# Weighing the values of two key tiles in a row in a causal attention stage

## The chip, the cores and the metric

One core of one Trainium2 chip. The metric is the device time of one execution in microseconds (us); the profiled execution has its own time, and its span runs from its first to its last instruction.

## The reference, cut to what matters

Sixteen-head causal attention over 4 sequences of 1024 tokens with 256 features (16 per head), a residual and a layer norm, then a mixture of 16 experts with two picks per token and a shared expert, a residual and a second norm. All of it is float32. The change touches the attention alone:

```python
q = split_heads(x @ Wq + bq)
k = split_heads(x @ Wk + bk)
v = split_heads(x @ Wv + bv)
scores = jnp.einsum('bhqd,bhkd->bhqk', q, k) / jnp.sqrt(jnp.float32(dk))
scores = jnp.where(causal[None, None], scores, -jnp.inf)
attn = jax.nn.softmax(scores, axis=-1)
out = jnp.einsum('bhqk,bhkd->bhqd', attn, v)
```

## The kernel before, in words

The kernel has three blocks, one after the other, each with its own instruction stream per engine: the projections to queries, keys and values (lines 377 to 577), the attention (lines 580 to 798), and all that follows (from line 812).

Attention runs in 16 steps: one per sequence (4) and group of four heads (4). A step works on two halves of 512 queries (`qc`), and each half on the key tiles of 128 that it may see (`kt`): 4 for the first half, 8 for the second. That makes 12 units (`UNITS`, line 39), numbered 0 to 11. Units 0 to 3 and 8 to 11 lie on the diagonal, so that their widths are 512, 384, 256 and 128 columns; units 4 to 7 are 512 wide.

For each unit there are

- the scores (line 722), in two pairs of heads: keys as weights, queries streaming, bfloat16, into PSUM banks 0 to 3, one bank per head. Every unit uses the same four banks, so a pair waits until the exp has read the same pair of the unit before (line 727);
- the exp on ScalarE (line 656), one activation per pair of heads, from PSUM into a slot of `probs` in SBUF. There are `PSLOTS` slots, and an exp waits until the weighing that last used its slot is done (line 659);
- for units on the diagonal the mask on GpSimd (line 628);
- the weighing (line 733): the probabilities stream, in float32, against the values of the four heads, each 32 columns wide (16 values and ones for the sum). Each head writes its own 32 partitions of bank 6, so the four run beside each other in the array; the trace shows this form as `128*32`. A half's weighings add up in bank 6, and then ScalarE copies them out (`copy_out`, line 666), TensorE turns the copy (`turn_out`, line 761) and VectorE divides by the sum (`normalise`, line 687).

The maximum that the exp subtracts is worked out one step ahead, beside this: TensorE computes the scores in a second arrangement, queries as weights (`piece_scores`, line 317, the matmuls of line 323 and on the diagonal the mask by line 326), and VectorE reduces each piece (`piece_maximum`, line 337). There are 38 pieces per step (`MAXES`, lines 45 to 51), numbered 0 to 37. When a half's pieces are reduced, VectorE splits the maxima into three bfloat16 parts (`max_parts`, line 349), TensorE turns these (`turn_maxima`, line 329), VectorE copies them (`copy_maxima`, line 344) and a DMA puts them as three further rows under the queries (`load_max`, line 370). Pieces and both kinds of turn share three PSUM banks, 4, 5 and 7, one after the other in the order in which they come (`RING_USERS`, line 94): each waits until the third one before it has been read (`ring_free`, line 748).

Each engine takes its own instructions strictly in order. TensorE's order in a step is written by `attention_order` (line 62): a chain of scores and weighings, in which the pieces of maxima are placed as their share of the cost comes due, and the turns are put behind certain items. VectorE takes the ring's users in the same order (line 698). A unit's weighing comes behind the next unit's scores. The last step has no next step, so it has neither pieces nor their turn for the first half (`present`, line 102). SyncE's queue carries `load_max` and the loads of queries and keys two steps ahead (line 600).

In memory, `probs` lies in `work` (line 581), and behind its three slots the third of three sets of values (line 296). The tensor `wgu` is free during the attention (its weights come later), and the third set of queries and keys and a block of zeros lie in it (lines 279 and 582).

Of the kernel before, what the change touches and what calls it, by code (L numbers as in the profile page):

```python
# [6 lines left out]
F32 = mybir.dt.float32  # L7
# [12 lines left out]
GH = 4  # L20
# [18 lines left out]
UNITS = [(qc, kt) for qc in range(HALVES) for kt in range(CT * (qc + 1))]  # L39
NU = len(UNITS)  # L40
DIAG = [u for u, (qc, kt) in enumerate(UNITS) if kt >= CT * qc]
PSLOTS = 3


MAXES = []
# [16 lines left out]
def attention_order():  # L62

    main = [("scores", 0, 0), ("scores", 0, 1), ("weigh", -1, 0)]
    for u in range(NU - 1):
        main += [("scores", u + 1, 0), ("scores", u + 1, 1), ("weigh", u, 0)]
    cost = [unit_width(u) * (2 if what == "weigh" else 1) for what, u, _ in main]  # L70
    pieces = [m[2] * m[4] + 60 for m in MAXES]
    order, n, done, spent = [], 0, 0, 0
    for item, c in zip(main, cost):
        order.append(item)
        if item == ("scores", 1, 1):
            order.append(("turn_max", 1, 0))
        if item == ("weigh", 1, 0):
            order.append(("turn_out", 1, 0))
        if item == ("weigh", 5, 0):
            order.append(("turn_out", 0, 0))  # L80
        done += c
        while n < NM and (spent + pieces[n] / 2) / sum(pieces) <= done / sum(cost):
            order.append(("max", n, 0))
            spent += pieces[n]
            n += 1
            if n == NM0 + TURN_AFTER:
                order.append(("turn_max", 0, 0))
    assert n == NM
    return order
# [113 lines left out]
def build(nc, x, xT, Wq, bq, Wk, bk, Wv, bv, Wo, bo, gate_w, expert_bias, sg_w, su_w, sd_w, gu_w, down_w, out):  # L203
    with ExitStack() as ctx:
# [87 lines left out]
                                 .rearrange("(h d) t -> d h t", d=DK)).then_inc(stack_loaded[r], 16)  # L292

        held = ctx.enter_context(ExitStack())
        vg = [held.enter_context(nc.sbuf_tensor(f"vg{r}", [P, NT, GH, 32], F32)) for r in range(2)]
        vg.append(work[:, 6144:7168].rearrange("p (t h e) -> p t h e", t=NT, h=GH))
        oT = [held.enter_context(nc.sbuf_tensor(f"oT{r}", [P, CH], F32)) for r in range(2)]
        mT = [held.enter_context(nc.sbuf_tensor(f"mT{r}", [3 * GH, CH], BF16)) for r in range(2)]
        recip = held.enter_context(nc.sbuf_tensor("recip", [P, CT, GH], F32))
        m_neg = held.enter_context(nc.sbuf_tensor("m_neg", [P, NT, GH], F32))  # L300
        m_neg_late = held.enter_context(nc.sbuf_tensor("m_neg_late", [P, CT, GH], F32))
# [278 lines left out]
        with ExitStack() as c2:  # L580
# [73 lines left out]
            @blk.scalar  # L654
            def _(act):
                def exp(i, u):
                    off = CH - unit_width(u)
                    s = (u % PSLOTS) * GH
                    wait_count(act, pv_done, NU * i + u - PSLOTS + 1)
                    for pair in range(2):  # L660
                        act.wait_ge(score_ready, 2 * (NU * i + u) + pair + 1)
                        act.activation(probs[:, s + 2 * pair:s + 2 * pair + 2, off:CH],  # L662
                                       ps[:, SCORE_BANK + 2 * pair:SCORE_BANK + 2 * pair + 2, off:CH],
                                       ACT.Exp, scale=float(DK) ** -0.5).then_inc(exp_done, 1)

                def copy_out(i, qc):
                    act.wait_ge(pv_done, NU * i + (CT if qc == 0 else NU))
                    wait_count(act, oT_ready, 2 * i + qc - 1)
                    act.activation(oT[qc][:, :], ps[:, OUT_BANK, :], ACT.Copy).then_inc(o_copied, 1)

                def step(i, prev=True):
                    for u in range(NU):
                        exp(i, u)
                        if u == 0 and prev:
                            copy_out(i - 1, 1)
                        if u == CT:
                            copy_out(i, 0)

                step(0, prev=False)
                step(1)  # L680
                with act.Fori(2, STEPS) as i:
                    step(i)
                copy_out(STEPS - 1, 1)
# [35 lines left out]
            @blk.tensor  # L719
            def _(pe):  # L720

                def scores(i, r, u, pair):
                    qc, kt = UNITS[u]
                    off = CH - unit_width(u)
                    if pair == 0 and kt == 0:
                        pe.wait_ge(m_loaded[qc], 48 * i + 48)
                    wait_count(pe, exp_done, 2 * (NU * i + u) + pair - 1)
                    for h in (2 * pair, 2 * pair + 1):
                        mm = pe.matmul(ps[:, SCORE_BANK + h, off:CH], ks[r][0:KM, h, kt * P:(kt + 1) * P],  # L729
                                       qs[r][0:KM, h, qc * CH + off:(qc + 1) * CH], start=True, stop=True)  # L730
                    mm.then_inc(score_ready, 1)

                def weigh(i, r, u):
                    qc, kt = UNITS[u]
                    off = CH - unit_width(u)
                    s = (u % PSLOTS) * GH
                    if u in DIAG:
                        pe.wait_ge(masked, len(DIAG) * i + DIAG.index(u) + 1)
                    else:
                        pe.wait_ge(exp_done, 2 * (NU * i + u) + 2)  # L740
                    if kt == 0:
                        wait_count(pe, o_copied, 2 * i + qc)
                    for h in range(GH):
                        mm = pe.matmul(ps[32 * h:32 * h + 32, OUT_BANK, off:CH], vg[r][:, kt, h, :],  # L744
                                       probs[:, s + h, off:CH], start=(kt == 0), stop=(kt == CT * (qc + 1) - 1))
                    mm.then_inc(pv_done, 1)

                def ring_free(i, item, first, last, second=False):

                    before, ago = ring_before(item, first, last, second)  # L750
                    if before is None:
                        return
                    what, n, _ = before
                    if what == "max":
                        wait_count(pe, reduced, NM * (i + 1 - ago) + n + 1)
                    elif what == "turn_max":
                        wait_count(pe, mT_copied[n], i + 2 - n - ago)
                    else:
                        wait_count(pe, a_written, 2 * (i - ago) + (1 if n == 0 else 0))

                def turn_out(i, qc):
                    pe.wait_ge(o_copied, 2 * i + qc + 1)
                    for t in range(CT):
                        mm = pe.transpose(ps[:, ring_bank(("turn_out", qc, 0)), t * P:(t + 1) * P],
                                          oT[qc][:, t * P:(t + 1) * P], ident[:, :])
                    mm.then_inc(oT_ready, 1)

                def step(i, k3, r, first=False, last=False, second=False):
                    pe.wait_ge(vg_ready, i + 1)
                    for item in ORDER:  # L770
                        what, n, pair = item
                        if item == ("max", 0, 0) and not last:
                            pe.wait_ge(stack_loaded[(r + 1) % STACKS], 192 * (k3 + (r + 1) // STACKS) + 192)
                        if what == "scores":
                            scores(i, r, n, pair)
                        elif what == "weigh":
                            if n >= 0:
                                weigh(i, r, n)
                            elif not first:
                                weigh(i - 1, (r - 1) % STACKS, NU - 1)  # L780
                        elif present(item, first, last):
                            ring_free(i, item, first, last, second)
                            if what == "max":
                                piece_scores(pe, i + 1, (r + 1) % STACKS, n, ring_bank(item))
                            elif what == "turn_max":
                                turn_maxima(pe, i + 1 - n, n, ring_bank(item))
                            else:
                                turn_out(i - n, n)

                step(0, 0, 0, first=True)  # L790
                step(1, 0, 1, second=True)
                pe.wait_ge(ones_ready, 2 * STACKS)
                for i in range(2, STEPS - 1):
                    step(i, i // STACKS, i % STACKS)
                step(15, 5, 15 % STACKS, last=True)
                weigh(STEPS - 1, 15 % STACKS, NU - 1)
                pe.wait_ge(a_written, 2 * STEPS - 1)
                turn_out(STEPS - 1, 1)

# [752 lines left out]
```

## Time and profile before

| | us |
|---|---|
| median of 3 runs | 989.87 (989.46 to 995.76) |
| the profiled execution, its own time | 996.05 |
| its span | 994.0 |
| TensorE busy in the span | 859.3 |
| VectorE busy | 643.4 |
| ScalarE busy | 474.3 |
| GpSimd busy | 341.1 |

The profile shows one execution. Times in it are counted from the span's start. The matmuls are pipelined: a matmul's record ends when its last result is through the array, later than the next one may start, so the distance between two starts, the pitch, is what a matmul costs its engine. The granted clock is the share of the TensorE clock's full speed.

### The profile page before, as it was taken

The numbers are of one execution on the slowest core, as the hardware profiler recorded it, in microseconds if no ns is written. First come the engines' busy times: TensorE is split into PE (matmuls) and PEld (weight loads), VectorE is DVE, ScalarE is ACT, GpSimd is POOL, SyncE is SP. The second block draws the span as 40 slices with busy tenths as digits, with TensorE's granted clock in tenths as the row PEclk, the third lists the DMA queues.
The fourth block names the chain that finished last, engine by engine and source line by source line (L and its number), as shares of the span: only waits on it lengthen the run. The fifth ranks groups of instructions, "written<-read, shape, count | busy, mean of one in ns | idle before, by whom it ended". The sixth has DMA issues, their size and how long they took to land. (4 is left out here: it accounts for less than half of the span.)

```text
span 994.0 us, 17348 instructions
## 1 busy us (share of the span) xinstructions
PE 859.3 (86%) x5476; PEld 482.8 (49%) x5477; DVE 643.4 (65%) x1527; ACT 474.3 (48%) x712; POOL 341.1 (34%) x450
## 2 busy tenths in 40 slices
PE   7979799999999999999999997978388669999910
PEld 4635444444444444444444426964157448878700
DVE  6428788888888888888888823882391112227655
ACT  3423366666666666666656673643112223444312
POOL 3513311221111221112211125637434655556732
PEclk9979899999999999999999998998598789999965
DMA  9874757555776556555224004602214434558563
GB/s 281 193 209 133 144 65 120 73 102 100 124 130 93 88 103 106 65 66 66 40 39 53 2 1 128 213 0 102 91 38 130 124 122 144 151 189 247 199 211 127
DMA packets 90410, 114.62 MB, mean 115 GB/s; under 512 B 9200, under 2 KB 70896, under 8 KB 90352
## 3 DMA queue, kind: packets, MB, share of 16 engines
q1 hardware_dynamic: 75728, 86.79, 41.5%
q0 software_dynamic: 7680, 21.11, 5.8%
q10 hardware_dynamic: 6944, 5.93, 1.9%
q8 instruction: 38, 0.62, 0.3%
q14 instruction: 20, 0.16, 0.1%
HBM read 62.74 MB, written 50.66 MB: 114 GB/s over the span
## 5 line engine op out<-in xcount | busy, mean ns | idle before, releaser
L662 ACT ACTIVATE work<-ps 128x1024 f32<-128x1024 f32 (+3 forms) x384 | 293.8, 811 | 180.0 <-PE ps L729 179.8
L341 DVE TENSOR_REDUCE m_neg<-ps 128x1 f32<-128x512 f32 (+3 forms) x432 | 265.2, 662 | 23.8 <-PE ps L326 13.4
L633 POOL TENSOR_SCALAR_AFFINE_SELECT work<-work 128x512 f32<-128x512 f32 x128 | 81.5, 637 | 386.5 <-ACT work L662 386.5
L323 PE MATMUL ps<-stacks 96*128 96x512 bf16 (+3 forms) x528 | 151.0, 330 | 1.5 <-DVE m_neg L341 1.5
L729 PE MATMUL ps<-stacks 99*128 99x512 bf16 (+3 forms) x528 | 124.7, 329 | 6.2 <-PEq L377 4.6
L341 DVE TENSOR_REDUCE m_neg_late<-ps 128x1 f32<-128x384 f32 (+3 forms) x176 | 106.7, 636 | 26.5 <-PE ps L326 26.5
L1029 POOL DMA_INDIRECT z_back<-stacks,home x96 | 93.4, 972 | 77.6 <-issue 30.6
L744 PE MATMUL ps<-work,vg 128*32 128x512 f32 (+3 forms) x1056 | 112.5, 498 | 1.5 <-POOL work L633 1.4
L1464 PE MATMUL ps<-wgu,work 128*128 x384 | 98.9, 404 | 8.6 <-issue 5.9
L1289 DVE TENSOR_TENSOR work<-work,ps 128x256 f32<-128x256 f32 x48 | 20.2, 420 | 130.3 <-ACT work L1111 101.4
L326 PE MATMUL ps<-mask_b,ident_b 128*128 128x128 bf16 x512 | 99.6, 221 | 0.0
L323 PEld LDWEIGHTS ps<-stacks 96*128 96x128 bf16 x528 | 49.6, 97 | 95.0 <-DVE m_neg L341 50.5
L1464 PEld LDWEIGHTS ps<-wgu,work 128*128 128x128 f32 x384 | 74.7, 205 | 19.2 <-issue 9.8
L1021 POOL DMA_INDIRECT y_sorted<-v_home,row_of x64 | 63.0, 984 | 43.4 <-DVE row_of L1256 23.9
L558 PE MATMUL ps<-work,wqk 128*128 128x512 f32 x128 | 63.5, 641 | 12.5 <-DMA work<-in_xT 7.0
L323 PE MATMUL ps<-wgu 96*128 96x512 bf16 (+3 forms) x240 | 68.8, 329 | 0.0
L729 PEld LDWEIGHTS ps<-stacks 99*128 99x128 bf16 x528 | 44.2, 98 | 43.8 <-ACT work L662 11.1
L447 POOL TENSOR_TENSOR work<-work 128x512 bf16<-128x512 f32 x32 | 36.7, 1156 | 71.6 <-ACT work L480 71.6
L729 PE MATMUL ps<-wgu 99*128 99x512 bf16 (+3 forms) x240 | 56.3, 325 | 0.0
L326 PEld LDWEIGHTS ps<-mask_b,ident_b 128*128 128x128 bf16 x512 | 50.7, 99 | 10.8 <-issue 2.5
L1480 PE MATMUL ps<-wdn,work 128*128 x192 | 51.1, 390 | 0.2
L744 PE MATMUL ps<-work 128*32 128x512 f32 (+3 forms) x480 | 51.1, 498 | 0.0
(142 smaller groups left out, 1075.8 us busy)
## 6 DMA issues: line engine op xcount, KB each, us to landing
stacks<-qk_parts SPq DMA_DIRECT2D x132, 128.0 KB, 6.4
y_sorted<-wgu SPq DMA_DIRECT2D x8, 1560.0 KB, 10.5
work<-y_sorted SPq DMA_DIRECT2D x48, 260.0 KB
qk_parts<-work SPq DMA_DIRECT2D x32, 384.0 KB, 2.9
work<-z_back SPq DMA_DIRECT2D x32, 256.0 KB
wgu<-qk_parts SPq DMA_DIRECT2D x60, 128.0 KB, 6.7
work<-in_xT SPq DMA_DIRECT2D x8, 512.0 KB, 5.3
work<-in_x SPq DMA_DIRECT2D x8, 512.0 KB, 4.2
```

Source lines behind the costliest of these rows:

```text
L323: mm = pe.matmul(dst, qs[r][0:KS, h0 + m, qt * P:(qt + 1) * P], ks[r][0:KS, h0 + m, half * CH:half * CH + w], start=True, stop=not diag)
L326: mm = pe.matmul(dst[:, w - P:w], ident_b[:, :], mask_b[:, :], start=False, stop=True)
L341: dve.tensor_reduce(dst, ps[:, bank, 0:heads * w].rearrange("p (h k) -> p h k", h=heads), AX.X, ALU.max, negate=True).then_inc(reduced, 1)
L558: mm = pe.matmul(ps[:, t, :], wqk[:, t // 2, h, (t % 2) * P:(t % 2 + 1) * P], xt[half][:, h, :], start=(h == 0), stop=(h == DC - 1))
L633: pool.affine_select(out=blk_, in_=blk_, compare_op=ALU.is_ge, fill=0.0, base=0, pattern=[[0, GH], [1, P]], channel_multiplier=-1).then_in ...
L662: act.activation(probs[:, s + 2 * pair:s + 2 * pair + 2, off:CH], ps[:, SCORE_BANK + 2 * pair:SCORE_BANK + 2 * pair + 2, off:CH], ACT.Exp, ...
L729: mm = pe.matmul(ps[:, SCORE_BANK + h, off:CH], ks[r][0:KM, h, kt * P:(kt + 1) * P], qs[r][0:KM, h, qc * CH + off:(qc + 1) * CH], start=Tr ...
L744: mm = pe.matmul(ps[32 * h:32 * h + 32, OUT_BANK, off:CH], vg[r][:, kt, h, :], probs[:, s + h, off:CH], start=(kt == 0), stop=(kt == CT * ...
L1021: pool.indirect_dma_start(out=y_sorted[g], out_offset=bass.IndirectOffsetOnAxis(ap=row_of[:, j, t:t + 1], axis=0), in_=y_rows_all[:, t, :] ...
L1029: pool.indirect_dma_start(out=z_back, out_offset=bass.IndirectOffsetOnAxis(ap=home[:, 2 * n + k:2 * n + k + 1], axis=0), in_=zs[n % ZS][:, ...
L1464: mm = pe.matmul(ps[:, 2 + r, 2 * F * k:2 * F * (k + 1)], ysT[r][:, h, k, :], wgu[:, bass.ds(e, 1), h, :].squeeze(1), start=(h == 0), stop ...
L1480: mm = pe.matmul(ps[:, 6 + r, D * k:D * (k + 1)], hxT[r][:, k, :], wdn[:, bass.ds(e, 1), :].squeeze(1), start=True, stop=True)
```

## The change

TensorE's order goes by pairs of units: the scores of units u and u+1, and then the weighings of units u-2 and u-1, one straight behind the other. No ring user is placed between the two weighings. So that exps of four units can be held, `probs` has four slots; the third set of values, which lay behind it, gets its own tensor, and the second output copy and the second buffer of turned maxima move into `wgu`. ScalarE's output copies come one exp later. What is left over at the end of a step is now two weighings, and the next step takes them.

```diff
-PSLOTS = 3
+PSLOTS = 4
...
-    main = [("scores", 0, 0), ("scores", 0, 1), ("weigh", -1, 0)]
-    for u in range(NU - 1):
-        main += [("scores", u + 1, 0), ("scores", u + 1, 1), ("weigh", u, 0)]
+    main = []
+    for u in range(0, NU, 2):
+        main += [("scores", u, 0), ("scores", u, 1), ("scores", u + 1, 0), ("scores", u + 1, 1),
+                 ("weigh", u - 2, 0), ("weigh", u - 1, 0)]
     cost = [unit_width(u) * (2 if what == "weigh" else 1) for what, u, _ in main]
     pieces = [m[2] * m[4] + 60 for m in MAXES]
     order, n, done, spent = [], 0, 0, 0
     for item, c in zip(main, cost):
         order.append(item)
+        done += c
+        if item[0] == "weigh" and item[1] % 2 == 0:
+            continue
         if item == ("scores", 1, 1):
             order.append(("turn_max", 1, 0))
...
-        done += c
         while n < NM and (spent + pieces[n] / 2) / sum(pieces) <= done / sum(cost):
...
-        vg = [held.enter_context(nc.sbuf_tensor(f"vg{r}", [P, NT, GH, 32], F32)) for r in range(2)]
-        vg.append(work[:, 6144:7168].rearrange("p (t h e) -> p t h e", t=NT, h=GH))
-        oT = [held.enter_context(nc.sbuf_tensor(f"oT{r}", [P, CH], F32)) for r in range(2)]
-        mT = [held.enter_context(nc.sbuf_tensor(f"mT{r}", [3 * GH, CH], BF16)) for r in range(2)]
+        vg = [held.enter_context(nc.sbuf_tensor(f"vg{r}", [P, NT, GH, 32], F32)) for r in range(STACKS)]
+        wgu_words = wgu[:, :, :, :].rearrange("p e c n -> p (e c n)")
+        oT = [held.enter_context(nc.sbuf_tensor("oT0", [P, CH], F32)),
+              wgu_words[:, GH * N + TRASHES * ROW:GH * N + TRASHES * ROW + CH]]
+        mT_at = GH * N + TRASHES * ROW + CH
+        mT = [held.enter_context(nc.sbuf_tensor("mT0", [3 * GH, CH], BF16)),
+              wgu_words[0:3 * GH, mT_at:mT_at + CH // 2].bitcast(BF16)]
...
                     for u in range(NU):
                         exp(i, u)
-                        if u == 0 and prev:
+                        if u == 1 and prev:
                             copy_out(i - 1, 1)
-                        if u == CT:
+                        if u == CT + 1:
                             copy_out(i, 0)
...
                             elif not first:
-                                weigh(i - 1, (r - 1) % STACKS, NU - 1)
+                                weigh(i - 1, (r - 1) % STACKS, NU + n)
...
-                weigh(STEPS - 1, 15 % STACKS, NU - 1)
+                for u in (NU - 2, NU - 1):
+                    weigh(STEPS - 1, 15 % STACKS, u)
```

Two places of TensorE's order in the second step (number 1) show what moves. Line numbers of after are 6 to 7 higher than those of before: L323 and L326 (a piece of maxima and its mask) are L329 and L332 there, L729 (scores) L735, L744 (weighing) L750, L764 (turn of the output) L770. A row with `x2` is one pair of heads.

The first place is units 8 and 9 (512 and 384 columns). TensorE before, from the first scores of unit 8 to the first scores of unit 9:

```order
L729 MATMUL ps<-stacks 128x512 x2
L323 MATMUL ps<-wgu 128x384
L326 MATMUL ps<-mask_b,ident_b 128x128
L729 MATMUL ps<-stacks 128x512 x2
L323 MATMUL ps<-wgu 128x384
L326 MATMUL ps<-mask_b,ident_b 128x128
L744 MATMUL ps<-work,vg1 32x512 x4
L323 MATMUL ps<-wgu 128x384
L326 MATMUL ps<-mask_b,ident_b 128x128
L323 MATMUL ps<-wgu 128x384
L326 MATMUL ps<-mask_b,ident_b 128x128
L729 MATMUL ps<-stacks 128x384 x2
```

TensorE after, from the same scores of unit 8 (its first row) to the double weighing of units 6 and 7 (its last):

```order
L735 MATMUL ps<-stacks 128x512 x2
L329 MATMUL ps<-wgu 128x512
L735 MATMUL ps<-stacks 128x512 x2
L329 MATMUL ps<-wgu 128x384
L332 MATMUL ps<-mask_b,ident_b 128x128
L735 MATMUL ps<-stacks 128x384 x2
L329 MATMUL ps<-wgu 128x384
L332 MATMUL ps<-mask_b,ident_b 128x128
L735 MATMUL ps<-stacks 128x384 x2
L329 MATMUL ps<-wgu 128x384
L332 MATMUL ps<-mask_b,ident_b 128x128
L750 MATMUL ps<-work,vg1 32x512 x8
```

Between the first scores of the two units stood the second pair, four pieces and a weighing; now the second pair and two pieces stand there, and the weighing comes behind both units.

The second place is the turn of the output of the step before, behind unit 1's weighing. TensorE before:

```order
L744 MATMUL ps<-work,vg1 32x384 x4
L764 MATMUL ps<-ident,oT1 128x128 x4
L323 MATMUL ps<-wgu 128x512
L326 MATMUL ps<-mask_b,ident_b 128x128
L729 MATMUL ps<-stacks 128x128 x2
L323 MATMUL ps<-wgu 128x512
L326 MATMUL ps<-mask_b,ident_b 128x128
L729 MATMUL ps<-stacks 128x128 x2
L744 MATMUL ps<-work,vg1 32x256 x4
```

And after, with the weighings of units 0 and 1 ahead of the turn:

```order
L750 MATMUL ps<-work,vg1 32x512 x4
L750 MATMUL ps<-work,vg1 32x384 x4
L770 MATMUL ps<-ident,wgu 128x128 x4
L329 MATMUL ps<-wgu 128x512
L332 MATMUL ps<-mask_b,ident_b 128x128
L329 MATMUL ps<-wgu 128x512
L332 MATMUL ps<-mask_b,ident_b 128x128
L329 MATMUL ps<-wgu 128x512
L332 MATMUL ps<-mask_b,ident_b 128x128
L329 MATMUL ps<-wgu 128x512
L332 MATMUL ps<-mask_b,ident_b 128x128
L735 MATMUL ps<-stacks 128x512 x2
```

Behind the turn two pieces stood with scores and a weighing among and behind them; now four pieces (7 to 10) stand there in a row, and then the scores of unit 4.

## Rows read from the trace of the kernel before

**Rows 1.** The page, busy tenths in 40 slices of the span.
```profile
PE   7979799999999999999999997978388669999910
PEclk9979899999999999999999998998598789999965
```

**Rows 2.** Stretches: start:end, length, then busy PE, PEld, DVE, ACT, POOL, clock, DMA.
```profile
513.25:543.54 30.29, 30.17 (x243) 12.95 (x241) 25.98 (x54) 19.18 (x26) 5.65 (x10) 1.00 0.44 54
573.85:598.41 24.56, 21.52 (x166) 6.31 (x164) 3.35 (x12) 18.87 (x26) 5.50 (x9) 1.00 0.00 1
640.00:700.00 60.00, 45.47 (x219) 33.60 (x217) 33.47 (x141) 23.20 (x35) 34.18 (x45) 0.86 0.21 73
```

**Rows 3.** Timeline (start, length, engine, line): first scores of two steps.
```profile
513.25 0.60 PE L729 MATMUL ps<-stacks 99*128 99x512 bf16 x2
...
543.54 0.60 PE L729 MATMUL ps<-wgu 99*128 99x512 bf16 x2
```

**Rows 4.** Timeline of TensorE around two weighings, of 128 and of 512 columns.
```profile
515.02 0.42 PE L744 MATMUL ps<-work,vg 128*32 128x128 f32 x8
515.38 0.28 PE L323 MATMUL ps<-wgu 96*128 96x256 bf16 x1
...
532.97 0.38 PE L323 MATMUL ps<-wgu 96*128 96x512 bf16 x1
533.28 1.07 PE L744 MATMUL ps<-work,vg 128*32 128x512 f32 x8
534.28 0.60 PE L323 MATMUL ps<-wgu 96*128 96x512 bf16 x2
```

**Rows 5.** Timeline, scores and exps: units 10 of step 13, then 4, 5 of step 15.
```profile
540.21 0.60 PE L729 MATMUL ps<-stacks 99*128 99x256 bf16 x4
540.63 1.08 ACT L662 ACTIVATE work<-ps 128x512 f32<-128x512 f32 x2 [1.00 <-PE ps L729]
...
581.31 1.04 PE L729 MATMUL ps<-stacks 99*128 99x512 bf16 x4
581.96 1.94 ACT L662 ACTIVATE work<-ps 128x1024 f32<-128x1024 f32 x2 [0.56 <-PE ps L729]
583.03 0.61 PE L729 MATMUL ps<-stacks 99*128 99x512 bf16 x2 [0.33 <-ACT work L662]
583.95 0.61 PE L729 MATMUL ps<-stacks 99*128 99x512 bf16 x2 [0.31 <-ACT work L662]
```

**Rows 6.** Timeline of TensorE, pitches of scores and of pieces of maxima.
```profile
528.50 0.38 PE L323 MATMUL ps<-wgu 96*128 96x512 bf16 x1
528.72 0.60 PE L729 MATMUL ps<-stacks 99*128 99x512 bf16 x2
529.16 0.63 PE L323 MATMUL ps<-wgu 96*128 96x512 bf16 x2
...
535.16 0.33 PE L323 MATMUL ps<-wgu 96*128 96x384 bf16 x1
535.38 0.59 PE L729 MATMUL ps<-stacks 99*128 99x512 bf16 x2
```

**Rows 7.** Timeline, four reductions and the piece that waits for the first of them.
```profile
528.66 2.47 DVE L341 TENSOR_REDUCE m_neg<-ps 128x1 f32<-128x512 f32 x4
529.39 0.10 PEld L323 LDWEIGHTS ps<-wgu 96*128 96x128 bf16 x1 [0.35 <-DVE m_neg L341]
```

**Rows 8.** Timeline: a turn of the output and its bank's next user; splitting the maxima.
```profile
530.71 0.66 PE L764 MATMUL ps<-ident,oT 128*128 128x128 f32 x4
531.21 0.27 PE L323 MATMUL ps<-wgu 96*128 96x256 bf16 x1
532.29 0.10 PEld L323 LDWEIGHTS ps<-wgu 96*128 96x128 bf16 x1 [0.30 <-DVE a_all L693]
...
544.46 0.18 DVE L355 TENSOR_TENSOR m_neg<-m_neg,m_neg_late 128x16 f32<-128x16 f32 x1
545.43 1.89 DVE L341 TENSOR_REDUCE m_neg<-ps 128x4 f32<-128x512 f32 x3
```

## The prediction

> **What bounds the kernel now.** I began with the busy tenths of the page. TensorE stands at 9 through the attention stage, slices 6 to 24, and its granted clock there is at or near full [rows 1]. Then I took stretches: one attention step lasts 30.29 us from its first scores to the next step's, TensorE is busy for 30.17 of them, VectorE for 25.98, ScalarE for 19.18, at clock 1.00 [rows 2, 3]. Fifteen steps (0 to 14) carry score maxima of the next step beside their own work; the last has none and takes 24.56 us [rows 2]. So TensorE in its own order sets the time of this stage, and the timeline of that engine is the view that matters: where it starts each thing, and whether the thing could have started earlier.
>
> A weighing of 512 columns starts 533.28 and the next matmul 534.28, so it holds the engine 1.00 us; one of 128 columns holds it 0.36 (515.02 to 515.38) [rows 4]. The difference, 0.64 for 384 columns, is the stream; what is left over, 0.15 us, is fixed. Ahead of it, the piece of maxima at 532.97 takes 0.22 (its pitch, [rows 6]) and would free the engine at 533.19, but the weighing starts at 533.28: another 0.09. So entering and leaving the four-column-group form costs 0.24 us per weighing, 2.9 us of each step. That is what the change is after.
>
> **What it saves.** Each step keeps its 12 weighings but has 6 entries in place of 12. If the second of two runs straight behind the first, 6 x 0.24 = 1.44 us go per step. No row shows two weighings in a row without a wait, so the bounds are 0 (the second pays as much as the first) and 1.44; I take 1.44, because the 8 matmul records of one weighing (two passes of four heads) already follow each other inside 1.07 us with one fixed cost [rows 4]. The Trainium skill, page "TensorEngine Tiling (Array Packing)", section "Key Properties", says that changing the tiling mode drains the engine; by that rule alone the saving would be the full 1.44, by the rows anything from 0 to it, and no run here shows the case yet.
>
> **What it costs: waits for the exps.** Scores live in four PSUM banks, one per head, so the first pair of heads of unit u+1 waits for the exp of that pair of unit u, and the second likewise. In the order before, a weighing and one to four maxima lie between, and no wait shows. In the new order the two units' scores stand side by side with only maxima between. How long the wait lasts can be read in the last step of the kernel before, which has no maxima: scores start 581.31, the exp 581.96, the next unit's first pair 583.03, its second pair 583.95 [rows 5]. So for 512 columns the next unit cannot start before 1.72 us and its second pair not before 2.64. For 256 columns the exp starts 0.42 after the scores (540.21, 540.63) and the two take 1.08, which gives releases at some 1.06 and 1.55 [rows 5].
>
> What TensorE has to do meanwhile: a pair of scores of 512 columns 0.44, a piece of maxima of 512 columns 0.22, one of 384 with its mask 0.22 [rows 6]; by columns, 384-wide scores are 0.33, 256-wide 0.22, 128-wide 0.11, a masked 512 piece 0.28, two masked heads of 256 columns 0.34, four of 128 0.47. Units by pairs:
> - 0, 1: 0.44 + 0.47 + 0.44 + 0.34 = 1.69 against 1.72, wait 0.03; second pair 1.72 + 0.33 + 0.34 = 2.39 against 2.64, wait 0.25.
> - 2, 3: 0.22 + 0.22 + 0.22 = 0.66 against 1.06, wait 0.40; second 1.17 against 1.55, wait 0.38.
> - 4, 5: 0.44 + 0.22 + 0.44 + 0.22 = 1.32 against 1.72, wait 0.40; the second pair stands behind a turn of maxima, no wait.
> - 6, 7: 0.40, then 2.60 against 2.64, 0.04.
> - 8, 9: 0.40, then 1.72 + 0.33 + 0.22 = 2.27 against 2.64, 0.37.
> - 10, 11: as 2, 3, 0.78.
> Together 3.45 us per step. Behind each waiting matmul stand all later instructions of TensorE; nothing overtakes it.
>
> **Waits for VectorE.** Maxima go round three banks, so a fourth piece in a row waits for the reduction of the first. The reduction frees the bank 0.73 us after it starts (528.66 to 529.39) [rows 7]. From the end of a pitch to the start of what waits for it some 0.20 pass: the exp at 581.96 starts 0.65 behind scores of 0.44 [rows 5, 6], and I take the same for VectorE, whose reductions follow each other at 0.62 (four in 2.47, [rows 7]). During a double weighing (0.88 to 1.95 us) no new piece comes, VectorE runs dry, and then pieces come four in a row at four places:
> - maxima 29 to 32: 0.22 + 0.20 + 0.62 = 1.04 against 0.66 of work, wait 0.38; 34 to 37: 0.28 + 0.20 + 0.73 = 1.21 against 0.84, wait 0.37.
> - 7 to 10 and 21 to 24 stand right behind a turn of the output. Its bank comes free 1.58 us after it starts (530.71 to 532.29) [rows 8], while TensorE has 0.50 + 0.56 to do: 0.52 at each place. The fourth piece waits for a reduction that VectorE starts only behind the normalising, at about 1.44, so free at 2.17: 0.31 and 0.37 more.
> - The chain that splits the maxima into parts holds VectorE 0.97 us (544.46 to 545.43) [rows 8]. Counted from the end of the double weighing ahead of 34 to 37, these keep VectorE until 2.9, the chain until 3.9, and the reduction of piece 0 frees its bank at 4.6; TensorE wants it for the first turn of maxima at 4.4 (1.49 for the four, 2.97 for units 0 and 1): 0.25 with the entry of that turn, and 0.22 at the piece behind it. Counted from the turn of the output ahead of 7 to 10, reductions start at 1.44 and end at 3.9, the chain (four operations here, so 0.78) at 4.65, and piece 11 frees its bank at 5.4, while TensorE wants it at 2.45 + 2.38 = 4.83: 0.54.
> Together 0.75 + 1.04 + 0.68 + 1.01 = 3.48 us per step. Bounds: 0, if the waits for the exps give VectorE the time it lacks, and about 5, if the late pieces push further ones.
>
> **What costs nothing.** Four slots of probabilities only let exps run one unit further ahead. One set of values, one output buffer and one of maxima change places in SBUF; the third set of queries and keys lies in the tensor they move into, and its pieces hold their pitch of 0.22 [rows 6], so I take 0 both ways. The copies of the output move one exp later on ScalarE, behind which the next unit's exp waits; by the walk each ends 0.1 to 0.3 before that exp's scores are there, and would cost about that if not. DMA queues see the same transfers about a microsecond later, with more than a step in hand.
>
> **Sum.** 3.45 + 3.48 - 1.44 = 5.49 us a step, 82.4 over 15 steps. The last step, without maxima, is walked by pairs: until the second unit's second pair is free (2.64 or 1.55), its own scores, the double weighing (0.24 + stream) and the turns behind it. That is 4.3 + 3.9 + 4.0 + 5.5 + 4.9 + 3.4, and 0.9 for the last weighings: 26.9 against 24.56, 2.3 more. In all 84.7: the profiled execution's 996.05 (span 994.0) would be 1080.7. The median of the runs, 989.87, is 6.2 under that execution, so I forecast 1074.6.
>
> **Rivals.**
> 1. Only the waits for the exps are real; in their shadow VectorE catches up. For it: VectorE is busy 25.98 of what would be 32 us. Against: it runs dry during the double weighings, which the average does not see. 1074.6 - 52.2 = 1022.
> 2. The second weighing pays its entry too, so nothing is saved: + 1.44 x 15 and about as much in the last step, 1098.
> 3. Faster: ScalarE frees each bank before TensorE asks, and only the saving is left, 95 double weighings x 0.24 = 22.8: 967. For it: ScalarE is busy only 19.18 of 30.29. Against: the wait is the latency of one exp, not its load. It decides if the second unit's scores start within 1.4 us of the first's; the rows say 1.72 [rows 5].
> 4. The gaps lower the clock. The last step, with gaps of 0.3 to 0.4, kept 1.00; the stretch from 640 to 700, busy 45.47 of 60, was granted 0.86 [rows 2]. At that level some 27.4 us of stream per step would take 4.5 longer: 72 more, 1146. The Trainium skill, page "TensorE: Matmul & The Clock Gate", section "A second HAM failure mode: psum-queue depth-cycling", tells of just such small idle times between groups of matmuls making the clock swing; the last step's row speaks against it here.
>
> **How the numbers follow.** The forecast has 0.58, with its own range 1055 to 1092; rival 1 has 0.14, rival 2 0.12, rival 4 0.08, rival 3 0.05, and 0.03 lies between rival 3 and rival 1, within 1% of now. A measurement of this kernel tells about 1% from no change. Faster 0.05, same 0.03, slower 0.92. The range takes in rivals 1 and 2: 1018 to 1104.
>
> **What would show it.** In the profile after: a step of about 35.8 us in the timeline; the second unit's scores 1.72 behind the first's, with idle time put down to the exp; fourth maxima idle behind the reduction; the two weighings of a pair as one block with one fixed cost; clock 1.00. A step of 32 us would mean rival 1; of 29, that the latency argument is wrong; a gap of 0.2 inside a double weighing, rival 2.

## Result, and the profile after

| | before | after |
|---|---|---|
| median, us | 991.27 (4 runs) | 1076.15 (4 runs) |
| ratio | | 1.0835, interval 1.0794 to 1.0876 |
| the profiled execution, its own time | 996.05 | 1075.42 |
| its span | 994.0 | 1073.3 |

The change makes the kernel 8.4% slower; the forecast was 1074.6. (The 989.87 ahead of the prediction is the median of three of the four executions of before.) The page's busy tenths of after, which answer to [rows 1], show where: TensorE falls from 9 to 8 throughout the attention stage, and the granted clock stays where it was.

```profile
PE   7899788888888888888888888797738787999820
PEclk9989899999999999999999999999859988999965
```

The next rows are stretches of after, one step from its first scores (510.00) to the next step's, and the last step; they answer to [rows 2], with the same columns.

```profile
510.00:545.74 35.74, 31.48 (x242) 13.23 (x241) 25.93 (x54) 19.03 (x26) 5.63 (x9) 1.00 0.36 46
652.98:679.94 26.96, 21.01 (x174) 7.38 (x172) 4.09 (x13) 18.60 (x26) 5.08 (x8) 1.00 0.00 1
```

A step takes 35.74 us where it took 30.29, and the last one 26.96 where it took 24.56. VectorE and ScalarE do the same work as before in it (25.93 and 19.03 us). TensorE's busy time is no measure of its waits here: a record ends when the last result is out, 0.16 us behind the pitch, so short gaps vanish under it (the piece at 519.26 below has a record of 0.38, and its pitch is 0.22). What counts is the distance between starts.

The timeline of TensorE after, units 8 and 9 and the double weighing of units 6 and 7:

```profile
534.40 0.60 PE L735 MATMUL ps<-wgu 99*128 99x512 bf16 x2
...
535.05 0.60 PE L735 MATMUL ps<-wgu 99*128 99x512 bf16 x2
...
536.11 0.50 PE L735 MATMUL ps<-wgu 99*128 99x384 bf16 x2 [0.24 <-ACT work L668]
...
537.02 0.50 PE L735 MATMUL ps<-wgu 99*128 99x384 bf16 x2 [0.19 <-ACT work L668]
...
537.68 1.92 PE L750 MATMUL ps<-work,vg 128*32 128x512 f32 x16
539.53 0.34 PE L329 MATMUL ps<-stacks 96*128 96x384 bf16 x1
```

Unit 9's scores start 1.71 us behind unit 8's (536.11 and 534.40) and their second pair 2.62, as read from the last step of before [rows 5]. The idle figure in the row of unit 9 (0.24) is smaller than the wait, since it counts from the end of a record; from pitch to start the two waits are 0.40 and 0.35. The double weighing holds TensorE 1.85 us (537.68 to 539.53) for two streams of 0.853, twice the 512 columns that [rows 4] give for one: one fixed cost of 0.15, and none between the two.

And the same engine around the turn of the output, with pieces of maxima (L329) and the second turn of maxima (L339):

```profile
518.76 0.66 PE L770 MATMUL ps<-ident,wgu 128*128 128x128 f32 x4
519.26 0.38 PE L329 MATMUL ps<-stacks 96*128 96x512 bf16 x1
...
520.45 0.39 PE L329 MATMUL ps<-stacks 96*128 96x512 bf16 x1 [0.47 <-DVE a_all L699]
...
521.04 0.39 PE L329 MATMUL ps<-stacks 96*128 96x512 bf16 x1
...
524.29 0.39 PE L339 MATMUL ps<-ident_b,m_parts 128*12 128x128 bf16 x4 [0.42 <-DVE m_neg L347]
```

Two pieces follow the turn at once; the third, at 520.45, waits 0.64 for the normalising, the fourth 0.31 for the first one's reduction, and the turn of maxima at 524.29 comes 0.59 late: it waits for a reduction behind the splitting of the maxima, and 0.09 of the 0.59 is its own entry, which before pays too.

### The profile page after: what moved, and what is told of

It is laid out like the page before. It is cut to its first block and busy times, and to the rows that moved or that the text cites. A ratio compares the mean times of both kernels' runs of the same rounds, so it can differ in the third digit from the quotient of the medians.

```text
span 1073.3 us, 17361 instructions
## 1 busy us (share of the span) xinstructions
PE 872.2 (81%) x5476; PEld 484.7 (45%) x5477; DVE 644.1 (60%) x1527; ACT 472.0 (44%) x712; POOL 339.4 (32%) x450
## 5 line engine op out<-in xcount | busy, mean ns | idle before, releaser
L668 ACT ACTIVATE work<-ps 128x1024 f32<-128x1024 f32 (+3 forms) x384 | 285.7, 812 | 247.0 <-PE ps L735 243.1
L329 PE MATMUL ps<-stacks 96*128 96x512 bf16 (+3 forms) x528 | 151.4, 330 | 19.4 <-DVE a_all L699 7.8
L735 PE MATMUL ps<-stacks 99*128 99x512 bf16 (+3 forms) x528 | 127.4, 331 | 30.3 <-ACT work L668 24.9
L750 PE MATMUL ps<-work,vg 128*32 128x512 f32 (+3 forms) x1536 | 143.6, 492 | 0.0
L332 PE MATMUL ps<-mask_b,ident_b 128*128 128x128 bf16 x512 | 100.1, 221 | 0.0
L329 PEld LDWEIGHTS ps<-stacks 96*128 96x128 bf16 x528 | 51.0, 98 | 98.3 <-issue 25.0
L329 PE MATMUL ps<-wgu 96*128 96x512 bf16 (+3 forms) x240 | 69.1, 329 | 9.3 <-DVE a_all L699 4.2
L735 PEld LDWEIGHTS ps<-stacks 99*128 99x128 bf16 x528 | 38.7, 98 | 81.5 <-ACT work L668 61.6
L750 PEld LDWEIGHTS ps<-work,vg 128*32 128x32 f32 x1536 | 40.4, 109 | 62.9 <-issue 47.9
L735 PE MATMUL ps<-wgu 99*128 99x512 bf16 (+3 forms) x240 | 57.6, 328 | 9.6 <-ACT work L668 9.2
L697 DVE RECIPROCAL recip<-ps 128x16 f32<-128x16 f32 x32 | 8.2, 257 | 85.4 <-PE ps L770 85.4
L332 PEld LDWEIGHTS ps<-mask_b,ident_b 128*128 128x128 bf16 x512 | 50.8, 99 | 10.7 <-issue 2.7
```

The source lines that it names most:

```text
L329: mm = pe.matmul(dst, qs[r][0:KS, h0 + m, qt * P:(qt + 1) * P], ks[r][0:KS, h0 + m, half * CH:half * CH + w], start=True, stop=not diag)
L332: mm = pe.matmul(dst[:, w - P:w], ident_b[:, :], mask_b[:, :], start=False, stop=True)
```

## The experiments

Eleven kernels ran. Two cuts return in several of them: "short reduce" lets VectorE read only 32 columns of each head of a piece, "short exp" lets ScalarE convert only 128 columns of a unit. The first leaves out the rest of the columns, the second the rest of the unit from the second step on, so that such a kernel does less than its task; both leave all matmuls, waits and orders as they are. What follows the attention can then work on other values, so these kernels are compared by their steps above all. The step in this table is the distance between two output copies of the same half, from each run's timeline. Each ratio is to executions of before that belong to the same group of runs (their medians: 991.27 for after, 994.47 for e1 to e3 and m2, 990.96 for m3 and e4 to e6, 996.05 for m4 and m6, 996.22 for m7). Rows of different groups compare by ratio and step, not by time.

| kernel | median, us | ratio to before | step, us |
|---|---|---|---|
| before | | 1 | 30.29 |
| after | 1076.15 | 1.0835 | 35.75 |
| e1, slots and memory only | 992.92 | 0.9989 (0.9956 to 1.0023) | 30.29 |
| e2, after, short reduce | 1040.57 | 1.0469 (1.0432 to 1.0506) | 33.37 |
| e3, after, short exp | 1052.06 | 1.0591 (1.0551 to 1.0631) | 34.12 |
| e4, after, both cuts | 991.82 | 1.0015 (0.9991 to 1.0040) | 30.57 |
| e5, before, both cuts | 984.76 | 0.9946 (0.9922 to 0.9969) | 30.06 |
| m2, pairs between the scores | 1024.15 | 1.0296 (1.0259 to 1.0333) | 31.96 |
| m3, turns ahead | 993.92 | 1.0031 (1.0011 to 1.0052) | 30.32 |
| e6, m3 with both cuts | 964.08 | 0.9740 (0.9699 to 0.9780) | 28.53 |
| m4, two narrow pairs | 987.36 | 0.9928 (0.9897 to 0.9958) | 29.86 |
| m6, three pairs | 987.99 | 0.9942 (0.9916 to 0.9968) | 29.94 |
| m7, three pairs, spread | 992.73 | 0.9962 (0.9934 to 0.9990) | 29.93 |

### e1: the slots and the memory alone

The kernel before, with two hunks of the change, of which these lines are a part:

```diff
-PSLOTS = 3
+PSLOTS = 4
...
-        vg.append(work[:, 6144:7168].rearrange("p (t h e) -> p t h e", t=NT, h=GH))
...
+              wgu_words[0:3 * GH, mT_at:mT_at + CH // 2].bitcast(BF16)]
```

> Memory and slots of the change alone (four slots of probabilities, the moved buffers), with the order of before. Theory (the whole loss is in the order of TensorE): no change, 991 us within 1%, and a step of 30.3 us. Rival (the moved buffers or the longer run-ahead of the exps cost something): above 1000 us.

No change, and the same step. So the loss is in the orders: that of TensorE, and that of ScalarE's copies, which e1 leaves where they were.

### e2 and e3: one engine's waits taken away at a time

```diff
-            dve.tensor_reduce(dst, ps[:, bank, 0:heads * w].rearrange("p (h k) -> p h k", h=heads), AX.X, ALU.max,
+            dve.tensor_reduce(dst, ps[:, bank, 0:heads * w].rearrange("p (h k) -> p h k", h=heads)[:, :, 0:32], AX.X, ALU.max,
```

> The changed kernel, but each reduction of a piece of maxima reads only the first 32 columns of each head, so VectorE is nearly always ahead. Theory (waits for VectorE are 3.5 us of a step, of which 1.05 are the latency of the normalising and stay): 2.5 us less per step, 37 us less, about 1038 us. Rival (only the exps hold TensorE, VectorE's waits lie in their shadow or move there): within 1% of 1076 us.

The step loses 2.37 us, and the time 35.6. TensorE's timeline in e2 still has the two kinds of waits that this cut cannot touch, the normalising and the exp:

```profile
494.70 0.39 PE L329 MATMUL ps<-stacks 96*128 96x512 bf16 x1 [0.47 <-DVE a_all L699]
...
496.98 0.61 PE L735 MATMUL ps<-wgu 99*128 99x512 bf16 x2 [0.25 <-ACT work L668]
```

The waits at fourth pieces and at the turns of maxima are gone. So they are real waits, not shadows of the exps' waits, and rival 1 falls.

```diff
-                        act.activation(probs[:, s + 2 * pair:s + 2 * pair + 2, off:CH],
-                                       ps[:, SCORE_BANK + 2 * pair:SCORE_BANK + 2 * pair + 2, off:CH],
+                        end = CH if isinstance(i, int) and i == 0 else off + P
+                        act.activation(probs[:, s + 2 * pair:s + 2 * pair + 2, off:end],
+                                       ps[:, SCORE_BANK + 2 * pair:SCORE_BANK + 2 * pair + 2, off:end],
```

> The changed kernel, but from the second step on each exp covers only the first 128 columns of its unit, so the next unit's scores are free after some 1.1 us in place of 1.72. Theory (waits for the exps are 3.45 us of a step and add to those for VectorE): some 0.9 us stay at the narrow units, 2.5 us less per step, about 1038 us. Rival (VectorE's ring takes up the time that is freed, since it is busy 26 of 36 us): at most half of that, 1057 us or more.

The step loses 1.63 us, between the two expectations. At the wide units the wait is gone: units 8 and 9 start 1.31 us apart in e3 (485.07 and 486.38), with no idle time between. The changed kernel and e3 have the same order of TensorE, so that their steps can be compared matmul by matmul: e3 gains 2.79 us at scores and gives 1.17 back at the two turns of maxima, which come 0.76 and 0.41 later than in after. The rows show the wide units and the first of these turns.

```profile
485.07 0.60 PE L736 MATMUL ps<-stacks 99*128 99x512 bf16 x2
...
485.72 0.60 PE L736 MATMUL ps<-stacks 99*128 99x512 bf16 x2
...
486.38 0.49 PE L736 MATMUL ps<-stacks 99*128 99x384 bf16 x2
...
498.86 0.39 PE L339 MATMUL ps<-ident_b,m_parts 128*12 128x128 bf16 x4 [0.82 <-DVE m_neg L347]
```

The scores ahead of it start at 497.55 and take 0.33, so the turn at 498.86 comes 0.98 late, where after has 0.23 at this place. One cast in the splitting ahead of it takes 0.46 longer than in after (last section), and that part is not the ring's. With this part, VectorE takes back part of what the exps free: the two sums of waits can be added for the order as it is, but not subtracted one by one.

### e4: both cuts on the changed kernel

The two edits above together.

> The changed kernel with both cuts: reductions of 32 columns per head, and exps of 128 columns from the second step on. Theory (e3 gained only 1.6 of 2.5 us per step because the ring of VectorE, above all the wait behind the splitting of the maxima, took up the rest): with both cut the exps' part is gained in full over e2, 2.5 us a step, 1002 us; the narrow units (0.8) and the normalising (1.1) stay. Rival (something else holds the order): 1020 us or more.

991.82, 10 us under what was expected. The step is 2.80 us under that of e2, nearly what stood at the scores (2.79). That makes 39 us over the 14 steps behind the first, whose exps are whole, and the last step, which waits for exps alone, lost 5.5 more (21.5 us against 27.0 in e2), which the expectation had left out. The step is still 2.04 us over that of e6: the normalising takes 0.64 and 0.53 of it from pitch to start, and four waits at the narrow units take 0.15 to 0.21 each.

### m2 and m3: the double weighing elsewhere

In m2 the two weighings stand between the scores of two units, and the pieces are placed by hand (`m` gives pieces of maxima, `tm` and `to` the turns; the places are behind each pair of scores and behind the weighings). Three of the six lines that place them in m2, and the line that builds the order:

```diff
...
+            (2, m(6), m(7), m(8, 9), m(10), [to[1]] + m(11)),
+            (4, m(12), m(13), m(14), m(15), [tm[0]] + m(16, 17)),
+            (6, m(18), m(19, 20), [], m(21), [to[0]] + m(22, 23)),
...
+        order += [S[2 * u]] + a + [S[2 * u + 1]] + b + pair(u - 2) + c + [S[2 * u + 2]] + d + [S[2 * u + 3]] + e
```

The same three lines in m3:

```diff
...
+            (2, m(5), m(6) + [to[1]], m(7), m(8), m(9, 10)),
+            (4, m(11), m(12), m(13), m(14), [tm[0]] + m(15, 16)),
+            (6, m(17), m(18) + [to[0]], m(19), m(20), m(21, 22, 23)),
...
```

> The double weighing is kept, but it stands between the scores of two units (u, then the weighings of u-2 and u-1, then u+1), and the pieces of maxima are placed by hand so that two or three stand ahead of each double weighing and two behind the second unit's scores. Theory (the double weighing saves its 1.44 us per step, and only the order of the scores costs): waits for the exps fall to about 0.5 us and those for VectorE to about 0.5 us per step, a step of 29.8 us, 984 us. Rival (double weighings starve VectorE wherever they stand): a step above 31 us, 1002 us or more.

The step is 31.96: the waits for the exps are nearly gone, but one wait alone is 1.44. The piece at 512.67 in m2 waits for the normalising of the turn at 509.31:

```profile
509.31 0.66 PE L764 MATMUL ps<-ident,wgu 128*128 128x128 f32 x4
...
512.67 0.39 PE L323 MATMUL ps<-stacks 96*128 96x512 bf16 x1 [1.29 <-DVE a_all L693]
```

I had put that turn behind the last piece of the first half, so the splitting of the maxima stood ahead of the normalising on VectorE. So 1024.15 lies where the rival put it, but much of it comes from my placing, as m3 shows.

> As m2_pairs_between, but the two turns of the output stand ahead of a double weighing, so that VectorE normalises during it, and one or two pieces are placed anew. In m2 one wait alone, for the normalising that had come behind the splitting of the maxima, was 1.44 us of a step. Theory (28.85 us of a step are TensorE's own work with double weighings, the rest is waits): a step of 29.3 to 29.8 us, 975 to 985 us. Rival (a double weighing starves VectorE, and this is given back elsewhere): 995 us or more.

That wait goes, the step is 30.32, and the kernel is 0.3% slower than before (interval 1.0011 to 1.0052). That is about 1% above the 975 to 985 of the theory and just under the rival's 995, so the theory lacks something. A step is level with one of before (30.29). The last step, in which no pieces stand, is not: it takes 28.6 us from its first scores to its last output copy, against 24.7 in before, which is more than the 3 us between the medians.

What m3 loses in a step shows beside e6 (below), which has the same order of TensorE and both cuts: m3 takes 1.79 us more, 1.33 of it ahead of pieces of maxima, 0.24 ahead of scores and most of the rest at the first turn of the output. So most of it stands at the ring. VectorE's timeline in m3 has these rows, the reductions behind four of the double weighings of a step:

```profile
475.73 1.57 DVE L341 TENSOR_REDUCE m_neg_late<-ps 128x1 f32<-128x384 f32 x3 [1.01 <-PE ps L326]
...
480.41 2.49 DVE L341 TENSOR_REDUCE m_neg_late<-ps 128x1 f32<-128x512 f32 x4 [0.71 <-PE ps L326]
...
489.79 2.48 DVE L341 TENSOR_REDUCE m_neg<-ps 128x1 f32<-128x512 f32 x4 [1.09 <-PE ps L326]
...
499.95 0.69 DVE L341 TENSOR_REDUCE m_neg<-ps 128x1 f32<-128x512 f32 x1 [0.99 <-PE ps L323]
...
```

Three banks hold three reductions, 1.86 us of work, and a double weighing with what comes ahead and behind keeps new pieces away for longer: VectorE stands idle for 3.8 us in these four rows (1.01, 0.71, 1.09 and 0.99), and then pieces in a row wait for it. It does not bound m3 by its work: that is 25.8 us of 30.32, with 4.5 idle, and in before, where TensorE hardly waits, VectorE is idle 4.3 of 30.28. The likely reading is that idle time of up to 1.1 us in one piece, in place of at most 0.7, is more than three banks can bridge. No run tried m3 with the reductions alone cut, or with more banks. The Trainium skill, page "TensorEngine Tiling (Array Packing)", section "PSUM Bottleneck", warns that tiling speeds TensorE up while the emptying of PSUM keeps its pace; m3 is another case, since VectorE has time to spare in it and lacks pieces at the right moment.

### e5 and e6: what a double weighing saves by itself

The kernel before, and m3, both with both cuts.

> The kernel before with the same two cuts. Theory (TensorE in the order before waits for nobody): 985 to 991 us. Rival (it has hidden waits too, so that comparing the waits of after alone overstates them): 975 us or less.

> The order of m3 with the same two cuts, so that with e5 only the form of the weighings differs. Theory (a double weighing saves 0.24 us): 95 of them, 22.8 us below e5_before_short_both, about 965 us. Rival (the second weighing pays its entry too): equal to e5.

With nobody to wait for, before takes 30.06 us per step and m3 28.53: 1.53 less for six entries, 0.25 each. By the distances between starts, 1.41 of it (0.24 each) stands where weighings begin and end, and 0.10 at the two turns of the output, which follow a weighing in e5 and not in e6. The times differ by 20.7 us. So the saving is real and about as large as the forecast had it; rival 2 falls. And before had only 0.23 us of waits per step that these cuts take away, so nearly all the waits of after are new.

### m4, m6 and m7: only as many pairs as VectorE bears

These take the order of before and move single weighings. m4 has two pairs, m6 a third, m7 two pieces placed anew. The first lines are m4's; behind the first mark stands what m6 changes in them, behind the second what m7 adds to m6. The lines for the two weighings left over at a step's end, as in the change, are left out:

```diff
+    order.remove(("weigh", 10, 0))
+    order.insert(order.index(("weigh", -1, 0)), ("weigh", -2, 0))
+    order.remove(("turn_out", 1, 0))
+    order.insert(order.index(("weigh", 1, 0)), ("turn_out", 1, 0))
+    for u in (2,):
+        order.remove(("weigh", u, 0))
+        order.insert(order.index(("weigh", u + 1, 0)), ("weigh", u, 0))
...
-    for u in (2,):
+    for u in (0, 2):
...
+    for n, behind in ((5, ("scores", 2, 0)), (6, ("scores", 2, 1))):
+        order.remove(("max", n, 0))
+        order.insert(order.index(behind) + 1, ("max", n, 0))
```

> The order of before, with three slots, and only two of the six pairs of weighings put together: units 2 and 3, and units 10 and 11 (streams of 0.64 us, shorter than one reduction more than the ring holds); the turn of the second half's output stands ahead of unit 1's weighing. Theory (an entry costs 0.24 us, and a short double weighing does not let VectorE's ring run dry): 0.48 us less per step, 7 us less than the kernel before, about 984 us. Rival (m3 gained nothing because a double weighing as such saves nothing on the whole): equal to the kernel before.

A little faster than before: ratio 0.9928 (0.9897 to 0.9958), 7 us. Its step is 29.86, 0.43 us under before, of 0.47 to 0.51 for two entries. The pair of units 2 and 3 in m4 stands between piece and scores, with nothing waiting behind it:

```profile
489.56 0.86 PE L751 MATMUL ps<-work,vg 128*32 128x256 f32 x16
490.35 0.61 PE L736 MATMUL ps<-stacks 99*128 99x512 bf16 x2
```

> As m4_two_narrow_pairs, with units 0 and 1 together too (a stream of 1.49 us), with four to five pieces of maxima ahead of them and the normalising during them. Theory: 0.72 us less per step than the kernel before if the ring keeps up, about 980 us; if the longer block starves VectorE, the third saving is given back: equal to m4_two_narrow_pairs or up to 4 us above it.

The third pair brings nothing more (0.9942, step 29.94). Without unit 0's weighing among them, four pieces follow each other behind a turn of maxima, and in m6 the third and the fourth come 0.21 and 0.23 us late:

```profile
482.22 0.33 PE L330 MATMUL ps<-stacks 96*128 96x384 bf16 x1
...
482.65 0.34 PE L330 MATMUL ps<-stacks 96*128 96x384 bf16 x1
...
483.12 0.34 PE L330 MATMUL ps<-stacks 96*128 96x384 bf16 x1
```

> As m6_three_pairs, whose step had two new waits of 0.21 and 0.23 us at pieces 5 and 6 (four pieces in a row once unit 0's weighing no longer stood among them); here piece 5 stands between unit 2's two pairs of scores and piece 6 behind them. Theory (the third pair's saving went into these two waits of the ring): they go, a step of 29.5 to 29.7 us, 0.6 to 0.8 us under that of before, 9 to 12 us less than the kernel before. Rival (the longer block starves VectorE and the waits reappear behind it): a step of 29.9 us as in m6.

The step stays at 29.93: the two waits go, and three of 0.13, 0.11 and 0.17 come at the next scores, the next piece and the turn of the output. In this stretch VectorE sets the pace: the splitting of the maxima has just held it for about a microsecond, and behind it no idle time above 0.05 us stands between its instructions for nearly 5 us, in m6 and in m7. The one other place tried for these pieces did not change that.

## Why the prediction was right

**What bounds the kernel.** Right. TensorE's order sets the stage, and the difference is there: step 0 takes 35.25 us against 31.55, steps 1 to 14 take 5.48 us more each, the last one 2.4 more. That is 82.8 us, against 84.7 forecast: the first step loses 3.7 where the forecast put 5.5, and the others agree. Outside the attention the two profiled executions differ by 3.5 us the other way, so that for the profiled execution the forecast (1080.7) is 5.3 above the 1075.42, while for the median it is 1.6 below. That the median was met so closely is in part luck; the agreement of the steps is the better evidence.

**The waits for the exps**, 3.45 us forecast, are 3.46 when the distances from pitch to start in one step of after are added: 0.04 and 0.24 at units 0 and 1, 0.41 and 0.38 at 2 and 3, 0.40 at 4 and 5, 0.40 and 0.04 at 6 and 7, 0.40 and 0.35 at 8 and 9, 0.42 and 0.38 at 10 and 11. They could be forecast this closely because the last step of before already showed the pattern without cover.

**The waits for VectorE**, 3.48 forecast, are 3.73 by the same addition: fourth pieces 0.38, 0.39, 0.31 and 0.38, the normalising 0.64 and 0.53, the turns of maxima 0.23, 0.28 and 0.59. The term that was short is the first place of the normalising, 0.64 for 0.52: the bank came free 1.69 us behind the start of the turn (518.76 to 520.45), where the place in [rows 8] had given 1.58. In these sums 0.09 is the entry of each of the two turns of maxima, which before pays too; the forecast had counted one of them, so the new waits are 3.55. e2 shows that they are not in the shadow of the other kind; e3 shows that the shadow exists once the exps are short.

**The saving**, 1.44, is 1.53 by e5 and e6, or 1.41 without the turns. The three terms now give 3.46 + 3.55 - 1.41 = 5.60, less the 0.23 of waits that before had: 5.37, where the steps differ by 5.46. So the terms account for the step within 0.1 us. The rule of the Trainium skill that the prediction weighed (page "TensorEngine Tiling (Array Packing)", section "Key Properties": a change of tiling mode drains the engine) is borne out on the side that the rows of before did not show: between two weighings of the same tiling nothing is lost, in the row of 1.85 us for two streams.

**What costs nothing.** Right: by e1 for slots and memory. The later copies on ScalarE have no run of their own, but they cost nothing that shows: at unit 3, whose scores wait for exps behind a copy, the waits are 0.41 and 0.38, and at unit 11, with no copy there, 0.42 and 0.38.

**The rivals.** Rival 1 falls by e2, rival 2 by e6. Rival 3 needed the second unit's scores within 1.4 us of the first's, and they stand at 1.71. Rival 4: the granted clock stayed at 1.00, the higher of its two levels (2.4 GHz), through steps with about 7 us of waits each (35.75 less the 28.53 of e6), so waits of this size and number (0.04 to 0.64 us each) did not lower it here. The Trainium skill, page "TensorE: Matmul & The Clock Gate", section "A second HAM failure mode: psum-queue depth-cycling", tells of small idle times between groups of matmuls making the clock swing; the granted clock of this step speaks against it for this kernel.

## What to carry to other kernels

Putting like work together to save an entry (0.24 us here) takes away what the interleaving hid: ask first how long the work between two users of a buffer must last (here 1.71 us from one unit's scores to the next, for one exp) and what the ring beside it can hold (three reductions, 1.86 us). A stage that lacks cover can show the price of a wait before the change is made, as the last step of this loop did. And a pairing can pay in part: the two narrow pairs (0.8 us of weighing each, against 1.86 in the ring) brought 0.7%, a third pair brought nothing more, and all six together nothing at all.

## What the runs showed of the hardware that I had not expected

A cast of 128x16 on VectorE, in the splitting of the maxima, takes 0.17 us where GpSimd does not work beside it. Where one starts during an instruction of GpSimd, it does not end before that instruction does: every slow one ends 0.03 us behind it, however long it is. In 15 steps of a run one cast takes 0.35 us in m4, m6 and m7, 0.43 in e6, 0.60 in e5, 0.62 in m2 and mostly 0.63 in e3. In the first step of every run one takes 2.42 beside a memset of 2.73; behind that step, before, after, e1, e2, e4 and m3 have no slow cast. Both engines in the timelines of e3 and of m4:

```profile
497.29 0.64 POOL L639 TENSOR_SCALAR_AFFINE_SELECT work<-work 128x512 f32<-128x512 f32 x1 [3.95 <-ACT work L669]
497.32 0.63 DVE L371 CAST m_parts<-m_rest 128x16 bf16<-128x16 f32 x1
...
489.16 0.61 POOL L320 COPY vg<-v_home 128x512 f32 x1
489.45 0.35 DVE L367 CAST m_parts<-m_neg 128x16 bf16<-128x16 f32 x1
```

In m2 GpSimd's partner is a copy (478.52, 0.61 us) and the cast starts at 478.54. The reciprocals of the normalising, which read PSUM, keep their 0.24 to 0.26 us beside a mask of GpSimd (e6, m3, m4). The slow cast added 0.46 us to the chain that splits the maxima, and so to the wait of 0.98 in e3 and to that of 1.44 in m2. The Trainium skill, page "GPSIMD Engine Reference", section "Specifications", says that GpSimd shares its SBUF interfaces with VectorE; these rows fit that, but that it is the cause was not tried, for instance by moving the mask alone.
